# A graph attention layer on one core: one block for all stages, a third of the tile-row gathers moved behind the edge loop, the marks moved behind the projection

## The chip, the core and the metric

The kernel runs on one NeuronCore of a Trainium2 chip. Its engines work in parallel and meet only at semaphores: TensorE (PE) multiplies, VectorE (DVE), ScalarE (ACT) and GpSimd (POOL) compute, SyncE (SP) issues transfers; ACT and POOL issue transfers too. Gathers by an index (indirect DMAs) are issued by GpSimd, one instruction for 128 rows. The metric is the device time of one execution in microseconds (us), as the median of several runs.

## What is computed

x holds 12,500 nodes of 128 features. There are 212,500 edges, sorted by their destination dst. Cut to what matters:

```
h = relu(layernorm(x))
q = h @ Wq.T + bq;  k = edge_attr @ Wk.T + bk;  v = h @ Wv.T + bv      # 8 heads of 16
qs, qd = q[src], q[dst]
score = (segsoftmax(qs.k) + segsoftmax(qd.k) + segsoftmax(qs.qd)) * edge_weight ** lam
out = x + leaky_relu(segment_sum(score * v[dst], dst) @ Wo.T + bo)
```

segsoftmax is a softmax over the edges of one destination. Since dst is sorted, the kernel computes it with running maxima and running sums along the edges, and reads each node's result at its last edge.

## The kernel before

There are three stages, each in a `Block` of its own: at the end of a block every engine waits until all have come.

**Node stage** (`node_pass`). The nodes are taken in 14 steps (NSTEP) of 7 tiles (HALF), two steps to a pair. VectorE takes the statistics of step k+3 (`node_stats`), finishes those of k+2 (`normalise`), and moves step k's q and v out of PSUM (`take_qv`); ScalarE normalises and copies the turned tiles, TensorE turns and projects, SyncE stores q and v to DRAM (`q_tab`, `v_tab`). Beside it runs a search: for each of 99 columns of 128 nodes it must be known where a node's last edge stands. `mark_tiles` finds the row of 128 destinations that holds it, GpSimd gathers these rows, 11 columns to a batch (`batch`, 9 batches, 99 gathers) into two buffers of `rows_i`, and VectorE counts in each batch (`count`, two instructions). A batch can only be fetched when the count two before it is done. `marks` compares neighbouring destinations and writes masks (`pen`), offsets (`near`) and, with ScalarE's logarithm and exponential, the edge weights (`att`); SyncE then writes `near_tab` and `pa_tab` to DRAM. `marks` stands after the third pair, counts after pairs 1 to 6 and at the end of the stage.

**Edge stage** (`edge_pass`). The edges are taken in 104 units of 4 groups, a group being 4 tiles of 128 edges. GpSimd gathers q of the sources (`qsrc`, 4 gathers to a group, 1,664 in all) into a ring of 8 groups, so it can be at most 8 groups ahead of TensorE's turn of them (`qs_turned`). SyncE loads edge features, offsets, masks and windows of q. TensorE, ScalarE and VectorE form the products, sum them over heads, and scan. Before the loop VectorE does the last two counts and works out with 22 small instructions (`place`) where every node's result stands (`last_i`). After it the ends of the 128 runs of edges are joined (`join_ends`, `join_fix`), and GpSimd gathers the 128 rows to be mended (`fix`) and scatters them back.

**Result stage** (`out_pass`). GpSimd gathers the results by `last_i`, 98 gathers in 14 steps into 4 buffers (`st`); VectorE scales v, TensorE applies Wo, ScalarE stores.

GpSimd's queue is one list in program order; an instruction in it that waits holds all behind it.

Of the kernel before, what the change touches and what calls it, by code (L numbers as in the profile page):

```python
# [54 lines left out]
NB = NN // LB  # L55
TINY = 2.0 ** -63
# [9 lines left out]
def gnn_kernel(nc, x, idx, dst_rows, dst_prev, dst_first, tile_first, ea, dist, wqvT, bqv, wkT, bk, woT, bo, lam,  # L66
# [12 lines left out]
    with ExitStack() as ctx:  # L79
# [15 lines left out]
        rows_i = sb("rows_i", [P, 2, LB * P], I32)  # L95
# [3 lines left out]
        rows_in = [sem("rows_in0"), sem("rows_in1")]  # L99
        rows_used = sem("rows_used")  # L100
        le_ready = sem("le_ready")
# [7 lines left out]
        def count(dve, m):  # L109

            dve.wait_ge(rows_in[m % 2], 16 * LB * (m // 2 + 1))
            need(dve, rows_used, m)
            nc.vector.tensor_tensor(le[:, :, :], rows_i[:, m % 2, :].rearrange("p (l i) -> p l i", i=P),
# [5 lines left out]
        node_pass(nc, locals())  # L119
        edge_pass(nc, locals())  # L120
# [3 lines left out]
def node_pass(nc, env):  # L124
# [4 lines left out]
    rows_i, rows_in, rows_used, idx, idx_sb, idx_in, count = (env[k] for k in (  # L129
        "rows_i", "rows_in", "rows_used", "idx", "idx_sb", "idx_in", "count"))  # L130
# [4 lines left out]
    with ExitStack() as ctx:  # L135
# [6 lines left out]
        def sem(name):  # L142
            return ctx.enter_context(nc.semaphore(name))

# [14 lines left out]
        mine = sb("mine", [P, T])  # L159
# [5 lines left out]
        tile_i = sb("tile_i", [P, NN], I32)  # L165
        dist_sb = sb("dist_sb", [P, T])
        clipped = sb("clipped", [P, T])
        power = sb("power", [P, T])
        keep = same
# [14 lines left out]
        bits = rows_i[:, :, :].rearrange("p b n -> p (b n)").bitcast(BF16)  # L184
# [22 lines left out]
        q_out = [sem("q_out0"), sem("q_out1")]  # L207
# [3 lines left out]
        bases_in = sem("bases_in")  # L211
# [5 lines left out]
        pool_turns = sem("pool_turns0")  # L217
# [3 lines left out]
        clipped_ready = sem("clipped_ready")  # L221
        pa_ready = sem("pa_ready")
        pa_out = sem("pa_out")
        zeros_out = sem("zeros_out")
# [4 lines left out]
        block = ctx.enter_context(nc.Block())  # L229

        @block.sync
        def _(sp):
# [5 lines left out]
            def store(k, b):  # L238
                sp.wait_ge(qv_copied, 2 * k + 2)
                sp.dma_start(q_v[:, bass.ds(k * HALF * F, HALF * F)], qs[:, b, :, :]).then_inc(q_out[b], 16)  # L240
                sp.dma_start(v_v[:, bass.ds(k * HALF * F, HALF * F)], vs[:, b, :, :]).then_inc(q_out[b], 16)
# [13 lines left out]
            sp.dma_start(bases[:, :], env["tile_first"]).then_inc(bases_in, 16)  # L255
            with sp.Fori(0, NSTEP // 2 - 3) as w:
# [6 lines left out]
            sp.wait_ge(zeros_ready, 1)  # L263
            sp.dma_start(q_tab[NPAD:NPAD + P, :], zeros[:, :]).then_inc(zeros_out, 16)
# [9 lines left out]
            sp.wait_ge(near_out, 16 * NSUP)  # L274
            sp.wait_ge(pa_out, 16 * A)
            sp.wait_ge(zeros_out, 16)
            for b in range(2):
                sp.wait_ge(q_out[b], 32 * (NSTEP // 2))
            sp.wait_ge(consts, 16 * NLOAD)
            sp.wait_ge(bases_in, 16)  # L280

        @block.scalar
        def _(act):
# [38 lines left out]
            with act.Fori(1, NSTEP // 2 - 1) as w:  # L322
# [5 lines left out]
                norm_relu(2 * w + 2, 0)  # L328
            copy_turned(NSTEP - 3, 1)
# [45 lines left out]
        def _(pool):  # L375
            def batch(m):
# [11 lines left out]
            for m in range(NB):  # L388
                batch(m)
# [967 lines left out]
```

## Time and profile before

| | |
|---|---|
| median of 3 runs | 2455.67 us (2454.73 to 2461.15) |
| the profiled execution | 2454.85 us, span of its trace 2453.0 us |
| node stage, to the first instruction of the next block | 0 to 177.3 us |
| edge stage | 177.3 to 2307.7 us |
| result stage | 2307.7 to 2453.0 us |
| busy: PE, DVE, ACT, POOL | 1788.6, 1731.4, 913.2, 1770.9 us |

The span is the time from the first to the last record of one profiled execution. An engine's busy share is an average over stages with different limits, so what a change is worth is read from the stage in which it stands and from the wait that ends last there.

### The profile page before, as it was taken

What the parts mean: (1) busy time and instruction counts of PE and PEld (TensorE: products, weight loads), DVE (VectorE), ACT (ScalarE), POOL (GpSimd) and SP (SyncE); (2) the same over time, 40 slices, a digit from 0 to 9 for tenths busy, and PEclk for the clock granted to TensorE, in tenths of its full rate; (3) what the DMA queues carried; (4) which work ended last, traced back from release to release, by engine and by line L of the source; (5) the groups of instructions that cost most, each with busy time, mean ns of one, the idle gap of its engine ahead of it and who ended that gap; (6) DMA issues with size and microseconds to landing.
All of it is one profiled execution on the core that took longest, in us unless ns stands there. A gap on an engine that the chain in (4) does not pass through costs nothing. (4 is left out here: it accounts for less than half of the span.)

```text
span 2453.0 us, 42538 instructions
## 1 busy us (share of the span) xinstructions
PE 1788.6 (73%) x10766; PEld 1111.6 (45%) x10766; DVE 1731.4 (71%) x2875; ACT 913.2 (37%) x1929; POOL 1770.9 (72%) x1869
## 2 busy tenths in 40 slices
PE   5406787877777777777777878777777777778177
PEld 4404444444444444444444444444444444444155
DVE  7736677777777777777777777777777777777355
ACT  5302343434334434333333434333343333334111
POOL 4567777777777777777777777777777777776374
PEclk9758888988888888888888888889888888889566
DMA  7468777777777777777777777777777777774254
GB/s 243 151 174 253 222 224 224 227 223 234 220 227 229 225 226 240 220 232 222 223 223 225 225 223 230 226 226 231 224 237 219 228 233 225 225 224 137 102 146 158
DMA packets 395523, 527.87 MB, mean 215 GB/s; under 512 B 82285, under 2 KB 301297, under 8 KB 382178
## 3 DMA queue, kind: packets, MB, share of 16 engines
q1 hardware_dynamic: 317586, 339.87, 44.3%
q0 software_dynamic: 59616, 119.35, 19.6%
q10 hardware_dynamic: 18288, 68.29, 7.6%
q8 instruction: 11, 0.18, 0.0%
q14 instruction: 22, 0.18, 0.0%
HBM read 442.67 MB, written 84.57 MB: 215 GB/s over the span
## 5 line engine op out<-in xcount | busy, mean ns | idle before, releaser
L718 POOL DMA_INDIRECT qsrc<-q_tab,idx_sb x1664 | 1576.8, 948 | 516.2 <-issue 497.9
L777 PE MATMUL qs_ps<-ident,qsrc 128*128 128x128 f32 x1664 | 306.2, 313 | 459.4 <-DMA qsrc<-q_tab,idx_sb 450.1
L941 DVE SCALAR_TENSOR_TENSOR prod<-k_ps,bk_col,kq 128x512 f32<-128x512 f32 x416 | 309.1, 743 | 464.3 <-PE lg_ps L747 442.2
L839 ACT COPY kq<-qd_ps 128x512 f32<-128x512 f32 x416 | 242.6, 583 | 901.0 <-PE qd_ps L768 895.3
L768 PE MATMUL qd_ps<-onehot,window 128*128 128x128 f32 x3328 | 525.3, 311 | 4.5 <-DVE onehot L931 4.5
L777 PEld LDWEIGHTS qs_ps<-ident,qsrc 128*128 128x128 f32 x1664 | 198.0, 155 | 725.7 <-issue 678.7
L757 PE MATMUL k_ps<-ea_sb,wk_sb 128*128 128x512 f32 x832 | 481.4, 664 | 55.3 <-DMA ea_sb<-in_ea 55.3
L945 DVE TENSOR_TENSOR prod<-qs_ps,kq 128x1024 f32<-128x1024 f32 x416 | 505.3, 1215 | 0.0
L768 PEld LDWEIGHTS qd_ps<-onehot,window 128*128 128x128 f32 x3328 | 490.4, 226 | 6.1 <-issue 6.1
L833 ACT ACTIVATE kq<-k_ps,bk_col 128x512 f32<-128x512 f32 x416 | 286.0, 688 | 213.0 <-PE k_ps L757 145.2
L747 PE MATMUL lg_ps<-prod,heads 128*32 128x384 f32 x3328 | 357.9, 503 | 1.5 <-DVE prod L945 1.5
L931 DVE TENSOR_SCALAR_CACHE_REDUCE onehot<-near_sb,node_col 128x512 f32<-128x512 bf16 x416 | 306.2, 736 | 0.0
L747 PEld LDWEIGHTS lg_ps<-prod,heads 128*32 128x32 f32 x3328 | 66.6, 109 | 358.2 <-issue 188.2
L788 PE MATMUL t_ps<-ident,sums 128*128 128x128 f32 x936 | 193.0, 324 | 14.9 <-ACT rows L863 12.1
L977 DVE TENSOR_TENSOR_SCAN sums<-max_ps,terms 128x387 f32<-128x387 f32 x208 | 189.0, 950 | 3.6
L757 PEld LDWEIGHTS k_ps<-ea_sb,wk_sb 128*128 128x128 f32 x832 | 147.9, 222 | 55.7 <-DMA ea_sb<-in_ea 55.7
L863 ACT COPY rows<-t_ps 128x384 f32<-128x384 f32 x312 | 148.4, 476 | 6.2 <-PE t_ps L788 6.2
L381 POOL DMA_INDIRECT rows_i<-in_dst_rows,tile_i x99 | 99.0, 1000 | 69.0 <-issue 54.0
L788 PEld LDWEIGHTS t_ps<-ident,sums 128*128 128x128 f32 x936 | 133.7, 167 | 27.1 <-issue 10.6
L1188 POOL DMA_INDIRECT st<-state,last_i x98 | 92.8, 947 | 38.8 <-issue 29.6
L956 DVE TENSOR_TENSOR_SCAN max_ps<-pa_sb,lg_ps 128x387 f32<-128x387 f32 x104 | 100.4, 965 | 25.1 <-ACT terms L846 24.6
L851 ACT COPY sums<-max_ps 128x387 f32<-128x387 f32 x104 | 50.0, 481 | 133.0 <-DVE max_ps L956 133.0
(147 smaller groups left out, 1034.9 us busy)
## 6 DMA issues: line engine op xcount, KB each, us to landing
ea_sb<-in_ea SPq DMA_DIRECT2D x104, 1024.0 KB
window<-q_tab SPq DMA_DIRECT2D x1664, 64.0 KB
state<-rows ACTq DMA_DIRECT2D x104, 576.0 KB
near_sb<-near_tab SPq DMA_DIRECT2D x104, 512.0 KB
pa_sb<-pa_tab SPq DMA_DIRECT2D x104, 258.0 KB
qsrc<-q_tab,idx_sb POOLq DMA_INDIRECT x1664
xs<-in_x SPq DMA_DIRECT2D x28, 448.0 KB, 5.4
q_tab<-qs SPq DMA_DIRECT2D x14, 448.0 KB, 2.7
```

The costliest lines, as they stand in the source:

```text
L718: pool.indirect_dma_start(out=qsrc[:, r, j, :], out_offset=None, in_=q_tab, in_offset=bass.IndirectOffsetOnAxis(ap=idx_sb[:, q, g * GRP + ...
L747: t = nc.tensor.matmul(lg_ps[2 * SUP * j:2 * SUP * (j + 1), :, 1:W1], heads[:, g, :], prod[:, m % 2, :, j * P:(j + 1) * P], start=g == 0, ...
L757: nc.tensor.matmul(k_ps[:, m % 2, :], wk_sb[:, :], ea_sb[:, p, g * GRP * P:(g + 1) * GRP * P], start=True, stop=True).then_inc(k_ready, 1)
L768: t = nc.tensor.matmul(qd_ps[:, at], window[:, r, j, :], onehot[:, m % 2, at], start=True, stop=True)
L777: t = nc.tensor.transpose(qs_ps[:, m % 2, j * P:(j + 1) * P], qsrc[:, r, j, :], ident[:, :])
L788: t = nc.tensor.transpose(t_ps[:, a * P:(a + 1) * P], sums[:, b, k, a, 1:W1], ident[:, :])
L833: nc.scalar.activation(kq[:, m % 2, 0, :], k_ps[:, m % 2, :], ACT.Identity, bias=bk_col[:, 0:1]).then_inc(k_copied, 1)
L839: nc.scalar.copy(kq[:, m % 2, 1, :], qd_ps[:, :]).then_inc(qd_copied, 1)
L931: nc.vector.tensor_scalar(onehot[:, m % 2, :].rearrange("p (j i) -> p j i", j=GRP), near_sb[:, p, :, :].rearrange("p (j g) i -> p g j i", ...
L941: nc.vector.scalar_tensor_tensor(out=prod[:, g % 2, 2, :], in0=k_ps[:, g % 2, :], scalar=bk_col[:, 0:1], in1=kq[:, g % 2, 1, :], op0=ALU.a ...
L945: nc.vector.tensor_tensor(prod[:, g % 2, 0:2, :], qs_ps[:, g % 2, :].unsqueeze(1).to_broadcast([P, 2, GRP * P]), kq[:, g % 2, :, :], ALU.m ...
L977: s = nc.vector.tensor_tensor_scan(sums[:, b, k, :, :].rearrange("p a i -> p (a i)"), max_ps[:, :, :].rearrange("p a i -> p (a i)"), terms ...
```

## The change

1. **One block.** All three stages stand in one `Block`. Instead of the two common ends each engine waits on named semaphores: SyncE, TensorE, ScalarE and VectorE wait in `nodes_done` (all of the node stage's work and stores, `pa_tab` included) before the edge stage, and in `edges_done` (results stored, ends joined, `fix` scattered, `edge_step` 40) before the result stage. GpSimd has waits of its own: only `q_out` (q is in DRAM) and `zeros_out` before the edge stage, and before the result stage `fix_out`, `edge_step` 20 and `rows_used` 6.
2. **Gathers.** `rows_i` has four buffers. Batches 0 to 5 (NEARLY = 6; 66 gathers) are fetched in the node stage, batches 6, 7 and 8 (33) behind the edge loop: 6 and 7 before the `fix` gather, 8 between that and the scatter. The result buffers `st` lie in the first two buffers of `rows_i`.
3. **Counts.** Counts 0 and 1 stand after pairs 3 and 4, counts 2 to 5 in the first four units of the edge loop, 6 before `join_ends`, 7 and 8 after `join_fix`. `place` is done in two parts: for 65 columns in the fourth unit, for 33 at the end.
4. **Marks** stand behind the last pair, with `near` and `clipped` earlier in them. `pa_tab` is written from ScalarE's queue, its first two parts before the logarithm. The zeros of `q_tab` are written early.
5. q and v stores have semaphores of their own (`q_out`, `v_out`).

The diff, cut to its core:

```diff
+NEARLY = 6
+BUF = (0, 1, 2, 3, 0, 1, 2, 3, 2)
+PLACED = NEARLY * LB - 1
...
+        def fetch_rows(pool, m, tile_i):
+
+            if BUF[m] in BUF[:m]:
+                pool.wait_ge(rows_used, max(k for k in range(m) if BUF[k] == BUF[m]) + 1)
+            pool.sem_inc(rows_turns, 1)
+            for j in range(LB):
+                pool.indirect_dma_start(out=rows_i[:, BUF[m], j * P:(j + 1) * P], out_offset=None, in_=dst_rows,
...
+        block = ctx.enter_context(nc.Block())
+
+        nodes_done = node_pass(nc, locals())
+        edges_done = edge_pass(nc, locals())
...
@@ node_pass, sync
-            sp.wait_ge(pa_ready, 3)
-            for a in range(A - 1):
-                sp.dma_start(pa_tab[:, :, a * W1:(a + 1) * W1], pa[:, :, 0, :]).then_inc(pa_out, 16)
-            sp.dma_start(pa_tab[:, :, (A - 1) * W1:], pa[:, :, :, :].rearrange("p c k i -> p c (k i)")
-                         ).then_inc(pa_out, 16)
...
@@ node_pass, scalar
+            act.wait_ge(pen_ready, 1)
+            act.wait_ge(pa_heads, 2)
+            for a in range(A - 1):
+                act.dma_start(pa_tab[:, :, a * W1:(a + 1) * W1], pa[:, :, 0, :]).then_inc(pa_out, 16)
             act.wait_ge(clipped_ready, 1)
             nc.scalar.activation(clipped[:, :], clipped[:, :], ACT.Ln).then_inc(ln_ready, 1)
             act.wait_ge(ln_ready, 1)
             nc.scalar.activation(power[:, :], clipped[:, :], ACT.Exp, scale=lam_sb[:, 0:1]).then_inc(power_ready, 1)
+            act.wait_ge(pa_ready, 1)
+            act.dma_start(pa_tab[:, :, (A - 1) * W1:], pa[:, :, :, :].rearrange("p c k i -> p c (k i)")
+                          ).then_inc(pa_out, 16)
...
@@ node_pass, gpsimd
-            for m in range(NB):
-                batch(m)
+            pool.wait_ge(tiles_ready, 2)
+            for m in range(NEARLY):
+                fetch_rows(pool, m, tile_i)
...
@@ node_pass, vector
             for w in range(1, NSTEP // 2):
                 pair(w, min(2, 2 * (NSTEP // 2 - 1 - w) - 1))
-                if w == 2:
-                    marks()
-                count(dve, w - 1)
-            dve.wait_ge(step, 18)
+                if w == 3 or w == 4:
+                    count(dve, w - 3)
+            marks()
+            dve.wait_ge(step, 17)
             dve.wait_ge(power_ready, 1)
             nc.vector.tensor_tensor(att, by_chunk(power[:, :]), by_chunk(keep[:, :]), ALU.mult).then_inc(pa_ready, 1)
-            count(dve, NB - 3)
...
@@ edge_pass, gpsimd
+            for b in range(2):
+                pool.wait_ge(env["q_out"][b], 16 * (NSTEP // 2))
+            pool.wait_ge(env["zeros_out"], 16)
             over_units(pool, unit)
 
+            for m in range(NEARLY, NB - 1):
+                fetch_rows(pool, m, tile_i)
             for b in range(2):
                 pool.wait_ge(rows_out[b], 16 * (NCOL // 2))
...
+            fetch_rows(pool, NB - 1, tile_i)
             pool.wait_ge(fixed_ready, 1)
...
+            pool.wait_ge(edge_step, 20)
+            pool.wait_ge(env["rows_used"], NEARLY)
             pool.wait_ge(fix_out, 16)
+            pool.sem_inc(pool_turns, 1)
+            for k in range(RST):
+                fetch_results(pool, k)
...
@@ edge_pass, vector
+                    if early and g == 2:
+                        count(dve, NEARLY - QUAD + q)
+                    if early and q == QUAD - 1 and g == 2:
+                        dve.wait_ge(env["rows_used"], NEARLY)
+                        place(0, PLACED, 0)
...
+            count(dve, NEARLY)
             join_ends()
             join_fix()
+            for m in range(NEARLY + 1, NB):
+                count(dve, m)
+            dve.wait_ge(env["rows_used"], NB)
+            place(PLACED, NT, 20)
```

**Where the instructions stand.** In the rows below each is one instruction, or a run of equal ones (x10), with its line and the semaphores that it waits for. First GpSimd from the last batch of the node stage to the first source gathers, before:

```order
L381 DMA rows_i<-in_dst_rows,tile_i 128x128 [waits tiles_ready,rows_used]
L381 DMA rows_i<-in_dst_rows,tile_i 128x128 x10
L135 UNCONDITIONAL_BRANCH
L707 UNCONDITIONAL_BRANCH [waits barrier_Pool_Activation_PE_DVE_SP_gather]
L718 DMA qsrc<-q_tab,idx_sb 128x128 [waits idx_in0]
L718 DMA qsrc<-q_tab,idx_sb 128x128 x15
```

and in the change (L138 is `fetch_rows`, L147 `fetch_sources`; line numbers are the changed kernel's):

```order
L138 DMA rows_i<-in_dst_rows,tile_i 128x128 [waits rows_used]
L138 DMA rows_i<-in_dst_rows,tile_i 128x128 x10
L755 UNCONDITIONAL_BRANCH
L147 DMA qsrc<-q_tab,idx_sb 128x128 [waits idx_in0,zeros_out,q_out0,q_out1]
L147 DMA qsrc<-q_tab,idx_sb 128x128 x15
```

The common end of the block between them is gone; the first source gather waits for the stores of q instead, and 33 row gathers that stood ahead of it do so no more.

Then GpSimd behind the edge loop, before, from the last source gathers to the first results:

```order
L718 DMA qsrc<-q_tab,idx_sb 128x128 x3
L728 DMA fix<-state,fix_i 128x72 [waits rows_out1,rows_out0]
L732 DMA state<-fixed,fix_i 212992x72 [waits fixed_ready]
L547 UNCONDITIONAL_BRANCH [waits fix_out]
L1181 UNCONDITIONAL_BRANCH [waits barrier_Pool_Activation_PE_DVE_SP_gather]
L1188 DMA st<-state,last_i 128x72 x28
```

and in the change, from the end of batch 6 on (L156 is `fetch_results`, its target lies in `rows_i`):

```order
L138 DMA rows_i<-in_dst_rows,tile_i 128x128 x10
L138 DMA rows_i<-in_dst_rows,tile_i 128x128 [waits rows_used]
L138 DMA rows_i<-in_dst_rows,tile_i 128x128 x10
L774 DMA fix<-state,fix_i 128x72 [waits rows_out1,rows_out0]
L138 DMA rows_i<-in_dst_rows,tile_i 128x128 [waits rows_used]
L138 DMA rows_i<-in_dst_rows,tile_i 128x128 x10
L779 DMA state<-fixed,fix_i 212992x72 [waits fixed_ready]
L156 DMA rows_i<-state,last_i 128x72 [waits fix_out,edge_step,rows_used]
L156 DMA rows_i<-state,last_i 128x72 x27
L1251 UNCONDITIONAL_BRANCH
L156 DMA rows_i<-state,last_i 128x72 [waits node_step1]
```

Batches 6 and 7 have come in ahead of the `fix` gather, batch 8 between that and the scatter; the common end behind the scatter is gone, and the first 28 result gathers follow it directly.

Last VectorE at the end of the node stage, before (two counts, the weights `att`, a third count, the common end), and at the start of the edge stage:

```order
L113 TENSOR_TENSOR le<-rows_i,nid 128x1408 [waits rows_used,rows_in1]
L117 TENSOR_REDUCE cnt<-le 128x11 [waits le_ready]
L535 TENSOR_TENSOR pa<-power,same 128x13x128 [waits power_ready,step]
L113 TENSOR_TENSOR le<-rows_i,nid 128x1408 [waits rows_used,rows_in0]
L117 TENSOR_REDUCE cnt<-le 128x11 [waits le_ready]
L135 UNCONDITIONAL_BRANCH
L919 UNCONDITIONAL_BRANCH [waits barrier_Pool_Activation_PE_DVE_SP_release]
L113 TENSOR_TENSOR le<-rows_i,nid 128x1408 [waits rows_used,rows_in1]
L117 TENSOR_REDUCE cnt<-le 128x11 [waits le_ready]
L113 TENSOR_TENSOR le<-rows_i,nid 128x1408 [waits rows_used,rows_in0]
L117 TENSOR_REDUCE cnt<-le 128x11 [waits le_ready]
L1104 SCALAR_TENSOR_TENSOR last_f<-tile_f,cnt 128x99 [waits rows_used]
```

and in the change, first where the node stage ends, then in the first unit of the edge loop:

```order
L546 CAST fix_i<-at_f 128x1 [waits step]
L569 TENSOR_TENSOR pa<-power,same 128x13x128 [waits power_ready,step]
L973 UNCONDITIONAL_BRANCH
L976 MEMSET held 128x8x3 [waits q_out1,v_out0,v_out1,q_out0,zeros_out,pa_ready,near_out,qv_copied,pa_out,hT_copied,h_ready]
L1000 TENSOR_TENSOR prod<-qs_ps,kq 128x1024 [waits qs_turned]
L126 TENSOR_TENSOR le<-rows_i,nid 128x1408 [waits rows_used,rows_in2]
L130 TENSOR_REDUCE cnt<-le 128x11 [waits le_ready]
L986 TENSOR_SCALAR onehot,picked<-near_sb,node_col 128x512 [waits qd_ready,near_in1]
```

VectorE now waits for the stores (`pa_out` among them) instead of the common end, and counts inside the loop's units, between the products and the next mask.

## Rows read from the trace of the kernel before

**Rows 1.** The page: busy time by engine; granted TensorE clock in 40 slices.
```profile
PE 1788.6 (73%) x10766; PEld 1111.6 (45%) x10766; DVE 1731.4 (71%) x2875; ACT 913.2 (37%) x1929; POOL 1770.9 (72%) x1869
...
PEclk9758888988888888888888888889888888889566
```

**Rows 2.** The page's costliest groups: line, engine, count, busy, mean ns, idle before.
```profile
L718 POOL DMA_INDIRECT qsrc<-q_tab,idx_sb x1664 | 1576.8, 948 | 516.2 <-issue 497.9
```

**Rows 3.** Windows, core 0: length, busy by engine, granted clock, DMA share, GB/s.
```profile
190.00:200.00 10.00, 5.71 (x30) 4.94 (x31) 6.68 (x14) 1.86 (x3) 7.56 (x9) 0.78 1.04 308
...
300.00:1000.00 700.00, 547.31 (x3395) 330.31 (x3395) 516.63 (x806) 278.34 (x596) 529.74 (x559) 0.86 0.75 226
```

**Rows 4.** Timeline of GpSimd: start, length, instruction, what ended the idle time.
```profile
88.87 2.25 POOL L381 DMA_INDIRECT rows_i<-in_dst_rows,tile_i  x1 [0.30 <-issue]
...
178.07 1.88 POOL L718 DMA_INDIRECT qsrc<-q_tab,idx_sb  x1 [9.15 <-POOLq L135]
...
181.50 1.83 POOL L718 DMA_INDIRECT qsrc<-q_tab,idx_sb  x1 [0.30 <-issue]
```

**Rows 5.** Timeline of GpSimd, end of the edge stage and start of the results.
```profile
2260.92 0.94 POOL L718 DMA_INDIRECT qsrc<-q_tab,idx_sb  x1 [0.30 <-issue]
2288.24 0.94 POOL L728 DMA_INDIRECT fix<-state,fix_i  x1 [26.38 <-DMA state<-rows]
2298.30 0.98 POOL L732 DMA_INDIRECT state<-fixed,fix_i  x1 [9.12 <-DVE fixed L1045]
2308.47 0.97 POOL L1188 DMA_INDIRECT st<-state,last_i  x1 [9.19 <-POOLq L547]
```

**Rows 6.** Timeline of VectorE in the node stage.
```profile
34.58 1.44 DVE L438 BATCH_NORM_STATS2 stats<-xs 128x6 f32<-128x128 f32 x7
...
45.32 1.61 DVE L113 TENSOR_TENSOR le<-rows_i,nid 128x1408 f32<-128x1408 int32 x1
...
48.50 1.44 DVE L438 BATCH_NORM_STATS2 stats<-xs 128x6 f32<-128x128 f32 x7
...
60.74 1.88 DVE L473 TENSOR_TENSOR same<-dst_i 128x1664 f32<-128x1664 int32 x1
...
73.57 1.62 DVE L113 TENSOR_TENSOR le<-rows_i,nid 128x1408 f32<-128x1408 int32 x1
...
88.69 1.62 DVE L113 TENSOR_TENSOR le<-rows_i,nid 128x1408 f32<-128x1408 int32 x1
...
107.96 1.44 DVE L438 BATCH_NORM_STATS2 stats<-xs 128x6 f32<-128x128 f32 x7
...
121.34 1.63 DVE L113 TENSOR_TENSOR le<-rows_i,nid 128x1408 f32<-128x1408 int32 x1
...
130.21 1.61 DVE L113 TENSOR_TENSOR le<-rows_i,nid 128x1408 f32<-128x1408 int32 x1
```

**Rows 7.** Timeline of SyncE's queue: issues, start and length.
```profile
138.43 3.65 SPq L272 DMA_DIRECT2D pa_tab<-pa  x1
177.32 0.37 SPq L679 DMA_DIRECT2D near_sb<-near_tab  x1
...
179.38 9.15 SPq L692 DMA_DIRECT2D window<-q_tab  x16
```

**Rows 8.** The tiles pa_tab, then q_tab, in the node stage: issue to landing.
```profile
DMA to landing us min/median/max: 7.9/14.0/19.5
...
DMA to landing us min/median/max: 2.5/2.7/4.2
```

**Rows 9.** Timelines of TensorE and VectorE as the edge stage begins.
```profile
184.52 2.08 PE L757 MATMUL k_ps<-ea_sb,wk_sb 128*128 128x512 f32 x2 [55.29 <-DMA ea_sb<-in_ea]
...
190.09 0.21 DVE L1099 CAST last_i<-edge_f 128x98 int32<-128x98 f32 x1
```

**Rows 10.** Timeline of ScalarE: logarithm and exponential of the distances.
```profile
122.09 1.28 ACT L335 ACT_TABLE_LOAD   x1
...
126.29 1.68 ACT L337 ACTIVATE power<-clipped,lam_sb 128x1664 f32<-128x1664 f32 x1
```

More of the change, by code:

```diff
@@ L94, in gnn_kernel @@
         cnt = sb("cnt", [P, NN])
-        rows_i = sb("rows_i", [P, 2, LB * P], I32)
+        qsrc = sb("qsrc", [P, RING, GRP, F])
+        q_in = [sem(f"q_in{r}") for r in range(RING)]
+        rows_i = sb("rows_i", [P, 4, LB * P], I32)
+        st = rows_i[:, 0:2, :].rearrange("p b n -> p (b n)").bitcast(F32)[:, 0:RST * HALF * ROW].rearrange(
+            "p (r t k) -> p r t k", r=RST, t=HALF)
+        st_in = [sem(f"st_in{r}") for r in range(RST)]
         le = sb("le", [P, LB, P])
@@ L98, in gnn_kernel @@
         idx_in = [sem(f"idx_in{q}") for q in range(QUAD)]
-        rows_in = [sem("rows_in0"), sem("rows_in1")]
+        rows_in = [sem(f"rows_in{r}") for r in range(4)]
         rows_used = sem("rows_used")
+        rows_turns = sem("rows_turns")
+        bases_in = sem("bases_in")
+        q_out = [sem("q_out0"), sem("q_out1")]
+        zeros_out = sem("zeros_out")
+        tile_i = sb("tile_i", [P, NN], I32)
         le_ready = sem("le_ready")
@@ L227, in node_pass @@
         zeros_ready = sem("zeros_ready")
-        block = ctx.enter_context(nc.Block())
+        block = env["block"]
         @block.sync
@@ L321, in _, with pair @@
             norm_relu(2, 0)
-            with act.Fori(1, NSTEP // 2 - 1) as w:
+            def pair(w):
                 copy_turned(2 * w - 1, 1)
@@ L328, in _ @@
                 norm_relu(2 * w + 2, 0)
+            with act.Fori(1, NSTEP // 2 - 1) as w:
+                pair(w)
             copy_turned(NSTEP - 3, 1)
@@ L603, in edge_pass @@
         pa_in = [sem(f"pa_in{q}") for q in range(QUAD)]
-        q_in = [sem(f"q_in{r}") for r in range(RING)]
         window_in = [sem(f"window_in{r}") for r in range(RING)]
@@ L671, in _ @@
         def _(sp):
+            env["nodes_done"](sp)
+            sp.wait_ge(env["bases_in"], 16)
             def unit(h, q):
@@ L803, in unit @@
                         sums_of_heads(h, q, g - 1)
+            env["nodes_done"](pe)
             keys(0, 0, 0)
@@ L896, in unit @@
                         exps(v)
+            env["nodes_done"](act)
             act.wait_ge(ones_ready, 3)
@@ L920, in _ @@
         def _(dve):
+            env["nodes_done"](dve)
             nc.vector.memset(held[:, :, 0, :], -BIG).then_inc(ones_ready, 1)
@@ L1046, in join_fix, with place @@
                                         ).then_inc(fixed_ready, 1)
-            def place(m0, m1):
+            def place(m0, m1, done):
+                c0, c1 = (m0 + 1 if m0 else 0), m1 + 1
+                nc.vector.scalar_tensor_tensor(out=last_f[:, c0:c1], in0=tile_f[:, c0:c1], scalar=float(P),
+                                               in1=cnt[:, c0:c1], op0=ALU.mult, op1=ALU.add).then_inc(step, 1)
+                dve.wait_ge(step, 2 if m0 else 1)
+                nc.vector.tensor_tensor(has[:, m0:m1], last_f[:, m0 + 1:m1 + 1], last_f[:, m0:m1], ALU.is_gt)
                 n = [edge_f[:, k, m0:m1] for k in range(8)]
@@ L1156, in out_pass @@
         pool_turns = sem("pool_turns2")
-        st_in = [sem(f"st_in{r}") for r in range(RST)]
         step = [sem(f"node_step{i}") for i in range(4)]
```

205 lines of the change are left out of this document (104 added, 101 removed).

## The prediction

> **What bounds the kernel now.** I read the page first. No engine is busy over 73% of the span [rows 1], so I asked which one never pauses where the time goes. The costliest group is GpSimd's 1,664 source gathers: 948 ns each, and the 516 us of idle time before them is "issue" in pieces of 0.30 us, not waiting [rows 2]. The timeline of GpSimd says the same: the first gather starts at 178.07 and the last at 2260.92 [rows 4, 5], so 1,663 steps took 2082.85 us, 1.2525 us each. A group of 4 gathers is 5.01 us, a unit 20.04 us. In the window from 300 to 1000 us, 34.9 units, TensorE was busy 547 us and VectorE 517 us [rows 3]: 15.7 and 14.8 us of each unit's 20.04. So **the edge stage lasts as long as GpSimd's issuing**, and the end of the kernel moves with the start of the first source gather, unless the others run so late that the ring of 8 groups fills.
>
> That gather started at 178.07 because the block had ended: the row gathers ran until 168.9, then GpSimd idled 9.15 us, released by the block's end [rows 4]. Behind the loop the chain is: last source gather ends at 2261.86 (call it E), `fix` at E+26.4, scatter at E+36.4 (VectorE's `fixed` released it), first result gather at E+46.6 after 9.19 us at the block's end [rows 5]; from there to the end of the span 144.5 us.
>
> **When the first source gather can start.** It now needs batch 5 issued and q stored.
> Pairs, from VectorE's timeline [rows 6]: pair 1 from 34.58 to 45.32, 10.74 us with no count ahead of it. A count takes 48.50 - 45.32 = 3.18. Pair 2 took 12.24 (48.50 to 60.74), pair 3 11.9 (from 73.57 + 3.18 to 88.69), pair 4 12.9 (from 88.69 + 3.18 to 107.96 - 3.18), pair 5 13.38, pair 6 5.69 (from 121.34 + 3.18 to 130.21), with a count ahead of each. `marks` took 73.57 - 60.74 = 12.83.
> New order: 45.32, pairs 2 and 3 like pair 1 (66.8), count 0 (70.0), pair 4 as after a count, 12.24 (82.2), count 1 (85.4), pair 5 at 13.38 (98.8), pair 6 between 5.69 and 8.87, since no count hides its wait for TensorE; I take 7.3. The projection ends at **106.1**. Bounds: all pairs at 10.74 and the short end, 100.3; each pair as slow as measured, 111.3. The last q store lands 2.7 us after its issue (2.5 to 4.2) [rows 8]; with 0.2 chosen for the semaphores q is there at 109.0.
> Batch 5 waits for count 1 (85.4) and takes 11 x 1.2525 = 13.8: done at 99.2, early enough; its slack is 10 us. The early zeros cost nothing here: they are hidden behind the projection.
> First source gather: **109.0 instead of 178.07, -69.1 us.**
>
> **Can the others follow?** Marks run from 106.1 to 118.9. ScalarE's logarithm and exponential took 5.88 from 122.09 to the end of the last [rows 10]; they start six instructions into marks and end about with them; `att` (1.9 us, as the equally long `same`, L473 [rows 6]) ends near 121.5. The last part of `pa_tab` then lands 7.9 to 19.5 us after its issue; 19.5 was behind the two other parts, which now go out some 10 us earlier, from ScalarE's queue [rows 7, 8]. I take 10: `nodes_done` at 131.5, bounds 129.4 and 141.0. From SyncE's first issue (177.32) to TensorE's first keys was 7.2 us (184.52), the keys took 2.08 [rows 7, 9]; with 2 us for mask, pick and turn, an estimate from the same row, group 0 is turned 11.3 us after `nodes_done`: **142.8** (140.7 to 152.3). GpSimd fills 8 groups in 32 x 1.2525 = 40.1 us, until 149.1. So it does not stall at the start by this estimate, by up to 3 us at the bound. SyncE's windows (9.15 us for a unit's 16 [rows 7]) are faster than 20 us.
> Then the first units carry counts: VectorE needs 14.8 + 3.2 = 18.0 us in each of three and 18.0 + 6.1 in the fourth (`place` took from 184.2 to 190.3, the end of L1099 [rows 9]; for 98 columns, so this is an upper bound for 65): 78 us against GpSimd's 80. The lead is kept and nothing is added. Where that cover is gone, each further microsecond of lateness costs one.
>
> **What slows GpSimd itself.** A row gather at 88.87 took 2.25 instead of 0.94 us [rows 4]: VectorE's compare of a count ran from 88.69 to 90.31 [rows 6], and the gather ended 0.81 us after it. Two source gathers at the start (1.88 and 1.83 us) lie beside the two counts there [rows 4]: 1.83 us lost, already in the 2082.85. All these instructions of VectorE read two tiles of SBUF. With such an instruction of 1.62 us a gather loses about 1.0, with one of 1.88 about 1.25. New beside source gathers: `near`, `mine`, `att` (3 x 1.25) and four counts (4 x 1.0), 7.75 - 1.83 = **+5.9**. Bounds: 0 and 11.
> The Trainium skill, SBUF — State Buffer, section Who interferes with whom, says that a VectorE instruction with two SBUF inputs contends only with a GpSimd instruction that reads SBUF, and infers that descriptor generation is not stalled by it; by that the sum would be 5.9 us lower. The row speaks against the inference.
>
> **Behind the loop.** Batches 6 and 7: 22 gathers, E+0.3 to E+27.9, plus 1.0 beside count 6, so `fix` at E+28.9 instead of E+26.4. The join does not feel it: its path goes over the ends that SyncE loads. `fix` and batch 8: 12 x 1.25 = 15.0, E+43.9, plus 1.0 beside count 7: the scatter at E+44.9 instead of E+36.4, though `fixed` is there at E+36.4. It ends at E+45.9. Its landing has no row of its own: the nearest are the q stores (2.5 to 4.2 from issue [rows 8]), the upper end is the whole 9.19 us that GpSimd sat at the block's end [rows 5]. I take 2.8: first result gather at E+48.7, **+2.1** (bounds +1 and +9). So the 9 us saved at this block's end are spent on batch 8.
> VectorE's count 8 waits for batch 8 (about E+47), then 3.2 and at most 6.1 for the second `place`: E+57. Only then do SyncE, TensorE, ScalarE and VectorE enter the result stage. The first step's 7 gathers are issued by E+57.5 anyway, and GpSimd needs the first buffer back at E+48.7 + 28 x 1.25 = E+83.8. Hidden by 20 us; the rest stays 144.5.
>
> **Sum.** -69.1 + 5.9 + 2.1 = -61.1. Span 2453.0 - 61.1 = 2391.9; the profiled execution had 1.85 us around its span and was 0.8 us below the median of the runs shown: 2391.9 + 1.85 + 0.8 = **2395 us**.
>
> **Rivals.**
> *The ring fills (0.14).* Group 0 is late and TensorE stays at its lower clock: the third slice of the page (123 to 184 us) has the granted clock at 5 tenths, its lower level, after a stretch in which TensorE had nothing to do [rows 1]; it was 0.78 from 190 to 200 and 0.86 later [rows 3]. TensorE's 3.92 us a group at 0.86 is at most 6.7 at 0.50; 16 groups would take 107 us against GpSimd's 80, so some 27 less the 6 to 9 of lead: +18, 2413. Against it: the same cold start recovered within 10 us.
> *The projection does not speed up (0.09).* Pairs as slow as with counts: 111.3 instead of 106.1, 2400.
> *The entry to the results is late (0.06).* The scatter's landing costs the full 9 us: +7, 2402.
> *No contention at the counts (0.04).* The gather beside a count would lose nothing: -5.9 -1 -1 = 2387. This is the mechanism of the page named above.
> *The start is early but worth nothing (0.03).* GpSimd fills the ring and waits for the same late `nodes_done` as before (177): then 2453 - 177.32 + 11.3 is the consumers' path and they catch up on the ring only: about the time of before, 2450 to 2458. It would take a `pa_tab` that lands 46 us late; its longest was 19.5.
> *Slower (0.02).* TensorE becomes the bound of the loop through its clock. 3.92 x 0.86 / c reaches 5.01 us at c = 0.673; the gain of 61 us over 416 groups is 0.147 a group, gone at c = 0.654. At 0.60 it is 5.62 us a group: +193 us net of the gain, about 2650. Nothing in the rows brings the clock of the loop down from 0.86.
>
> **How the numbers follow.** The forecast has 0.62, with a range of its own from 2386 (projection at 100.3, half the contention) to 2404 (projection at 111.3, some 4 us later behind the loop). A difference of 0.3%, 7.4 us, is about what a measurement of this kernel can tell from none. Faster: 0.62 + 0.14 + 0.09 + 0.06 + 0.04 = 0.95. Same: 0.03, the start worth nothing. Slower: 0.02. The range goes from 2384 (early projection, little contention) to 2413 (the ring fills).
>
> **What would show it.** The first source gather near 109, with one gap before it and none at a common end; `nodes_done` 20 us later; GpSimd's gathers without gaps over 0.4 us from then to the last, at about 2198; seven gathers of 1.6 to 2.8 us by the early counts and marks; the scatter at E+45, the first result at E+49. It is wrong if GpSimd waits for TensorE's turns around 150 us, if the mean of a gather rises above 0.95 us, or if the result stage is longer than 145 us.

## The result, and the profile after

The changed kernel took **2396.32 us** (median of 4 runs, 2391.21 to 2402.75), the kernel before 2456.81 us beside it (4 runs, 2454.73 to 2461.15). The ratio is 0.9753, with a 95% interval from 0.9725 to 0.9781: faster by 60 us, where 61 less were predicted (2395). Measured again in a later set of runs it was 2398.25 us (2394.02 to 2402.97) against 2454.67, ratio 0.9769 (0.9749 to 0.9790). Eight of the experiments ran on two chips on which the kernel before itself took 3269.51 and 3327.28 us, so their totals are compared only with those.

The profiled execution took 2398.02 us, its span was 2396.2 us, 56.8 less than before. The page has the same work in a shorter span; the third slice of the granted clock, 5 tenths before [rows 1], is 7:

```profile
PE 1795.9 (75%) x10766; PEld 1111.0 (46%) x10766; DVE 1734.8 (72%) x2897; ACT 914.0 (38%) x1929; POOL 1778.5 (74%) x1869
...
PEclk9878988888888988989888888888888888888566
```

GpSimd's three lists of gathers among the costliest groups (line, engine, count, busy, mean ns, idle before; answers to [rows 2]):

```profile
L147 POOL DMA_INDIRECT qsrc<-q_tab,idx_sb x1664 | 1586.3, 953 | 516.7 <-issue 502.0
...
L138 POOL DMA_INDIRECT rows_i<-in_dst_rows,tile_i x99 | 96.8, 978 | 49.2 <-issue 29.3
...
L156 POOL DMA_INDIRECT rows_i<-state,last_i x98 | 93.1, 950 | 31.7 <-issue 29.6
```

The 516.7 us of idle time are the same 0.30 us pieces as before. What moved is when the list starts. GpSimd's timeline at the end of batch 5, the first source gathers, and the last one (answers to [rows 4]):

```profile
101.98 0.95 POOL L138 DMA_INDIRECT rows_i<-in_dst_rows,tile_i  x1 [0.30 <-issue]
112.41 0.95 POOL L147 DMA_INDIRECT qsrc<-q_tab,idx_sb  x1 [9.48 <-DMA q_tab<-qs]
113.66 2.14 POOL L147 DMA_INDIRECT qsrc<-q_tab,idx_sb  x1 [0.30 <-issue]
116.11 1.46 POOL L147 DMA_INDIRECT qsrc<-q_tab,idx_sb  x1 [0.30 <-issue]
117.87 1.50 POOL L147 DMA_INDIRECT qsrc<-q_tab,idx_sb  x1 [0.30 <-issue]
...
122.18 2.63 POOL L147 DMA_INDIRECT qsrc<-q_tab,idx_sb  x1 [0.31 <-issue]
...
2204.97 0.95 POOL L147 DMA_INDIRECT qsrc<-q_tab,idx_sb  x1 [0.30 <-issue]
```

VectorE beside it (answers to [rows 6]): the marks begin at 109.03, so there the projection ends. `near`, `mine` and `att` (the lines L510, L520 and L569) are the three instructions beside which slow gathers were foreseen. The slow gather at 116.11 is a fourth: it begins while L518 runs, an instruction with one input in SBUF, and ends 0.82 us after it. The first source gather, at 112.41, begins while L509 runs and is not slow. After `att` VectorE waits 11.87 us for `pa_tab`.

```profile
109.03 1.88 DVE L506 TENSOR_TENSOR same<-dst_i 128x1664 f32<-128x1664 int32 x1
...
111.00 1.89 DVE L509 TENSOR_SCALAR pa<-same 128x1664 f32<-128x1664 f32 x1
112.81 1.88 DVE L510 TENSOR_TENSOR near<-dst_i 128x1664 bf16<-128x1664 int32 x1
...
115.72 1.03 DVE L518 TENSOR_SCALAR dist_sb<-dist_sb 128x1664 f32<-128x1664 f32 x1
116.67 1.88 DVE L520 TENSOR_TENSOR mine<-dst_i,nfirst 128x1664 f32<-128x1664 int32 x1
...
122.09 1.89 DVE L569 TENSOR_TENSOR pa<-power,same 128x1664 f32<-128x1664 f32 x1
135.85 0.08 DVE L976 MEMSET held<- 128x24 f32 x1 [11.87 <-DMA pa_tab<-pa]
```

And the start of TensorE's part (answers to [rows 9]):

```profile
143.53 2.04 PE L809 MATMUL k_ps<-ea_sb,wk_sb 128*128 128x512 f32 x2 [35.48 <-DMA ea_sb<-in_ea]
...
147.07 1.10 PE L829 MATMUL qs_ps<-ident,qsrc 128*128 128x128 f32 x8
```

Group 0 is turned about 148.1. The 33rd source gather, the first that needs a group's place in the ring again, starts at 156.38 after the usual 0.30 us. The others began 36 us behind GpSimd and it did not wait for them.

Behind the loop, GpSimd (answers to [rows 5]); E is now 2205.92:

```profile
2227.88 2.05 POOL L138 DMA_INDIRECT rows_i<-in_dst_rows,tile_i  x1 [0.30 <-issue]
...
2235.23 0.95 POOL L774 DMA_INDIRECT fix<-state,fix_i  x1 [0.31 <-issue]
...
2243.99 2.12 POOL L138 DMA_INDIRECT rows_i<-in_dst_rows,tile_i  x1 [0.30 <-issue]
...
2251.41 0.98 POOL L779 DMA_INDIRECT state<-fixed,fix_i  x1 [0.30 <-issue]
2254.53 0.97 POOL L156 DMA_INDIRECT rows_i<-state,last_i  x1 [2.14 <-DMA state<-fixed,fix_i]
```

`fix` at E+29.3, scatter at E+45.5, first result at E+48.6. The scatter waits for nothing: `fixed` was written by 2243.75 (E+37.8), and batch 8 stood ahead of it in the list.

The balance of the two spans: first source gather 112.41 instead of 178.07, -65.66; the 1,663 steps from first to last source gather 2092.56 instead of 2082.85 us, +9.71; from the last source gather to the first result 49.56 instead of 47.55, +2.01; from there to the end 141.67 instead of 144.53, -2.86. Sum -56.8.

### The profile page after: what moved, and what is told of

The parts are those of the page before. It is cut to its first block, busy times and chain, and to the rows that moved or that the text cites. A ratio compares the mean times of both kernels' runs of the same rounds, so it can differ in the third digit from the quotient of the medians.

```text
span 2396.2 us, 42567 instructions
## 1 busy us (share of the span) xinstructions
PE 1795.9 (75%) x10766; PEld 1111.0 (46%) x10766; DVE 1734.8 (72%) x2897; ACT 914.0 (38%) x1929; POOL 1778.5 (74%) x1869
## 3 DMA queue, kind: packets, MB, share of 16 engines
q0 software_dynamic: 59616, 119.35, 20.2%
## 4 chain that ended last, share of the span: by engine, by line
POOL 58%; issue 20%; PE 10%; DVE 5%; DMA 5%; ACT 1%; POOLq 1%; ACTq 0%; DVEq 0%; SPq 0%
POOL qsrc L147 53%; DMA qsrc<-q_tab,idx_sb 3%; POOL rows_i L156 3%; PE qd_ps L820 2%; PE k_ps L809 2%; POOL rows_i L138 1%; PE lg_ps L799 1%; PE qs_ps L829 1%; PE qv_ps L394 1%; DVE prod L1000 1%; PE t_ps L840 1%; ACT hb L334 1%; DMA pa_tab<-pa 0%; POOLq L66 0%; DVE prod L996 0%
## 5 line engine op out<-in xcount | busy, mean ns | idle before, releaser
L147 POOL DMA_INDIRECT qsrc<-q_tab,idx_sb x1664 | 1586.3, 953 | 516.7 <-issue 502.0
L1000 DVE TENSOR_TENSOR prod<-qs_ps,kq 128x1024 f32<-128x1024 f32 x416 | 505.3, 1215 | 0.0
L138 POOL DMA_INDIRECT rows_i<-in_dst_rows,tile_i x99 | 96.8, 978 | 49.2 <-issue 29.3
L1011 DVE TENSOR_TENSOR_SCAN max_ps<-pa_sb,lg_ps 128x387 f32<-128x387 f32 x104 | 100.3, 965 | 30.9 <-ACT terms L899 28.6
L156 POOL DMA_INDIRECT rows_i<-state,last_i x98 | 93.1, 950 | 31.7 <-issue 29.6
```

The costliest lines, as they stand in the source:

```text
L147: pool.indirect_dma_start(out=qsrc[:, r, j, :], out_offset=None, in_=q_tab, in_offset=bass.IndirectOffsetOnAxis(ap=idx_sb[:, q, g * GRP + ...
L1000: nc.vector.tensor_tensor(prod[:, g % 2, 0:2, :], qs_ps[:, g % 2, :].unsqueeze(1).to_broadcast([P, 2, GRP * P]), kq[:, g % 2, :, :], ALU.m ...
```

## The experiments

### Does the end move one for one with the first source gather?

The theory of the prediction: GpSimd's list sets the time, so a later first source gather costs what it is late. The rival: GpSimd's early start only fills its ring, and the time hangs on when the other engines start. Four edits move one against the other. In the first GpSimd waits for the whole node stage, as the others do:

```diff
-            for b in range(2):
-                pool.wait_ge(env["q_out"][b], 16 * (NSTEP // 2))
-            pool.wait_ge(env["zeros_out"], 16)
+            env["nodes_done"](pool)
             over_units(pool, unit)
```

> The changed kernel, but GpSimd waits for all of the node stage (nodes_done, pa_tab included) before the source gathers, like the other engines. Theory (the start of the first source gather sets the end): it starts near 136.2 instead of 112.4 us, +23.8, and no longer meets the three long VectorE instructions of marks (3.9 us lost beside them in the changed kernel's trace): +19.9, about 2416 us. Rival (the other engines' start at 135.8 sets the pace of the loop and the ring only hides it): no change, 2396.

The second does `marks()` after the third pair (`if w == 2`), as before, in place of behind the last:

> The changed kernel with marks back after the third pair, all else kept. Theory: the projection ends some 13.5 us later (marks took 12.8 us, and the pipeline refills), so the first source gather is near 126; near and mine no longer meet source gathers: -2.3. In all about +11, 2407 us. nodes_done hardly moves (near 134). Rival (the start of the other engines sets the time): no change, 2396.

The third fetches and counts all 9 batches ahead of the edge loop, and nothing behind it:

```diff
-            for m in range(NEARLY):
+            for m in range(NB):
                 fetch_rows(pool, m, tile_i)
...
-                    if early and g == 2:
-                        count(dve, NEARLY - QUAD + q)
...
-            for m in range(NEARLY, NB - 1):
-                fetch_rows(pool, m, tile_i)
```

> The changed kernel with all nine batches of row gathers and all counts ahead of the edge loop, still in one block. Theory: batch 8 has to wait for count 6 and ends near 148, so the first source gather starts near 148.7 instead of 112.4, +36; no count lies in the loop, -2.6; behind the loop nothing stands between fix and scatter, the first result gather comes at E+39.9 instead of E+48.6, -8.7: about +25, 2421 us. If batch 8 behind the loop costs nothing there (rival), the last term is missing: about 2430.

The fourth delays only the others, by 8 reductions of VectorE behind the marks, ahead of `att`:

```diff
+            for i in range(8):
+                nc.vector.tensor_reduce(nfirst[:, 0:1], mine[:, :], AX_X, ALU.add).then_inc(step, 1)
+                dve.wait_ge(step, 18 + i)
             dve.wait_ge(power_ready, 1)
```

> The changed kernel with eight more reductions (1.89 us each, 15.1 us, one SBUF input) on VectorE ahead of att, so that all but GpSimd enter the edge stage 15 us later. In the changed kernel GpSimd's gather into the first slot of the ring that has to be free again starts at 156.4, the slot was free at 148.1: 8.3 us of cover. Theory: the excess over the cover shows, +7, about 2403 us. Rival 1 (no cover is left in later units, one for one): +15, 2411. Rival 2 (the ring is never full): 2396.

These four ran where the kernel before took 3269.51 us (31 runs): 3264.44, 3274.49, 3254.65 and 3257.56 us (10 runs each), ratios 0.9975 (0.9938 to 1.0012), 1.0034 (1.0003 to 1.0065), 0.9961 (0.9926 to 0.9995), 0.9979 (0.9956 to 1.0001). All four expectations (2396 to 2421 us) missed by over 800 us, and not through the edits: the kernel before, unedited, was as slow there. The changed kernel itself was not run on that chip. In the first one's list of costliest groups GpSimd's idle time is 1245.4 us, of which only 457.3 are its own pace; the largest part of the rest, 381.0 us, is put down to the loads of the gathers' indices (`idx_sb`), which SyncE issues:

```profile
L147 POOL DMA_INDIRECT qsrc<-q_tab,idx_sb x1664 | 1577.0, 948 | 1245.4 <-issue 457.3
```

and a stretch of its chain that ended last (start, length, what) has a hole of the length of half a unit:

```profile
1041.17 0.66 DVE onehot L984 x2
1041.83 9.62 another core or an unknown queue
1051.48 0.05 DVEq L66
```

From 1049.9 to 1051.5 none of TensorE, VectorE, ScalarE and GpSimd is at work in this trace; VectorE had stood since 1041.8, ScalarE since 1043.1, TensorE since 1046.3. From 300 to 1000 us GpSimd issued 416 source gathers, a unit in 26.9 us instead of 20. So GpSimd was not what bounds the loop there. In that condition the first source gather came at 181.96, 181.48, 204.22 and 162.90 in the four, and the time did not follow: the one with the latest start has the lowest median. Nor did it follow the start of the others: VectorE's `held`, its first instruction of the edge stage, came at 181.13, 192.29, 212.11 and 198.42, and again the latest has the lowest median. So these four runs decide nothing between theory and rival; what bounds the loop there stays open.

The changed kernel and the first edit were therefore run again together:

> The changed kernel itself, beside the kernel before on the same chip. Two earlier sets of runs had the kernel before at 3270 and 3327 us instead of 2457, with TensorE, VectorE, ScalarE and GpSimd at rest together for some 10 us in each unit of the edge loop. If this chip is like the one of the result: 2396 us, ratio 0.975, first source gather at 112. If it is like those: GpSimd is not the engine that sets the loop there, so an early first gather only fills its ring; the ratio should be 0.994 to 1.000 and the first source gather near 163.

> As the first experiment: before its first source gather GpSimd waits for all of the node stage (pa_tab and near_tab too), not for q alone. If this chip is like the one of the result and my theory holds (the end moves one for one with the first source gather): the gather starts at about 136 instead of 112, hence 2396 + 24 less the slow gathers beside near, mine and att (3 x 1.25) = 2416 us, ratio 0.983. Rival: TensorE's start sets the loop, and GpSimd's early start is cover only: 2396, ratio 0.975. If the chip is like the two others: 0.994 to 1.000 whatever the theory.

Here the kernel before took 2454.67 us. The changed kernel took 2398.25 us (0.9769). With the wait for the whole stage it took **2414.16 us** (2409.70 to 2416.69), ratio 0.9825 (0.9809 to 0.9842). GpSimd's timelines, of the change and of this one:

```profile
110.83 0.94 POOL L147 DMA_INDIRECT qsrc<-q_tab,idx_sb  x1 [9.51 <-DMA q_tab<-qs]
```

```profile
132.42 0.94 POOL L147 DMA_INDIRECT qsrc<-q_tab,idx_sb  x1 [30.75 <-DMA pa_tab<-pa]
```

21.6 us later at the start; 4.8 less in the steps (4.0 of it because the plain step is 1.2485 instead of 1.2509 us, and only 0.8 from slow gathers, where I had expected 3.75); 0.4 less behind the loop; 3.8 more in the result stage; together +20.2, the difference of the spans (2414.8 and 2394.6). The others started 2.4 us earlier here than in the change (VectorE's `held` at 131.59 and 133.95), and the kernel is slower all the same. That refutes the rival: it gives 2396, and all four runs lie above 2409. The closeness to the expected 2416 is partly luck: the plain step (-4.0) and the result stage (+3.8), neither of which the expectation had, cancel.

The third edit was also run again, with the numbers worked out anew:

> The change without its moved gathers: all 9 batches are fetched ahead of the edge loop, and all counts stand in the node stage; one block, named waits and marks behind the projection stay. If this chip is like the one of the result and GpSimd's list sets the time: 33 more gathers stand ahead of the first source gather, 41 us, of which the 9.5 us that it waits for q hide some, and each batch has to wait for a count; the first source gather starts at about 160, with the counts out of the loop's way. Behind the loop fix waits for the join and the scatter comes at E+36 instead of E+45, the first result at E+40 instead of E+49. 2398 + 48 - 9 - 4 less contention = 2433 us, ratio 0.991 (from the first set I had said 2421, before I had the waits between batches). Rival: the moved gathers gave nothing, since they cost behind the loop what they save ahead of it: 2398, ratio 0.977. If the chip is like the two slower ones: within 1% of the kernel before.

It took **2424.27 us** (2423.65 to 2425.01) against 2456.80, ratio 0.9872 (0.9855 to 0.9888). GpSimd's timeline:

```profile
156.14 0.94 POOL L147 DMA_INDIRECT qsrc<-q_tab,idx_sb  x1 [0.30 <-issue]
...
2266.46 0.94 POOL L774 DMA_INDIRECT fix<-state,fix_i  x1 [26.31 <-DMA state<-rows]
2276.53 1.00 POOL L778 DMA_INDIRECT state<-fixed,fix_i  x1 [9.13 <-DVE fixed L1103]
2279.67 0.97 POOL L156 DMA_INDIRECT rows_i<-state,last_i  x1 [2.14 <-DVE edge_i L1146]
```

Against the changed kernel beside the other set: start +45.3, steps -9.7, to the first result -9.0, result stage +1.1, sum +27.7, again the difference of the spans (2422.3 and 2394.6). So the 33 moved gathers are worth 26 us: ahead of the loop they cost 45.3 us, less 9.7 since neither counts nor marks are left to stand beside source gathers (5.6) and the plain step is short again (4.0); behind it they cost 9.0, because 26 us of GpSimd's waiting for the join cover most of them there. Without the 4.0 us of the plain step, which nothing here explains, they would be worth some 30. My second estimate had counted 48 us for the start and only 4 for the steps and was 9 too high; the first, 2421, was nearer. What remains without them, 2456.8 - 2424.3 = 32.5 us, is the share of all that this version keeps: the single block, the named waits, the marks behind the projection, the four buffers and the moved stores of `pa_tab` and the zeros. The parts of these 32.5 us were not told apart, since the second and fourth edit ran only where GpSimd is not the bound.

### What slows a gather beside VectorE?

Theory: a gather that stands beside a VectorE instruction with two inputs in SBUF ends only after it. Rival, an inference of the Trainium skill, SBUF — State Buffer, section Who interferes with whom: the generation of descriptors is not held up by such an instruction. Two kernels put one more instruction of VectorE into each of the 100 units after the first four, equally long, with two inputs in SBUF or with one:

```diff
+                    if not early and g == 1:
+                        nc.vector.tensor_tensor(le[:, :, :], rows_i[:, 1, :].rearrange("p (l i) -> p l i", i=P),
+                                                nid[:, 0:LB].unsqueeze(2).to_broadcast([P, LB, P]), ALU.is_le)
```

> The changed kernel with one more compare of VectorE (two SBUF inputs, 1.62 us, the same as in a count) in each of the last 100 units of the edge loop; its result is not used. VectorE has 5 us free in a unit of 20. Theory (GpSimd cannot begin a gather while such an instruction runs): a gather that falls into it loses on average 0.87 us (between 0.24 and 1.49), so +87 us, about 2483 (2420 to 2545). Rival (the inference that descriptor generation is not stalled by a two-input tensor_tensor): 2396.

```diff
+                    if not early and g == 1:
+                        nc.vector.tensor_reduce(spare[:, :], le[:, :, :], AX_X, ALU.add)
```

> The control to the run with a compare in each unit: there one more reduction of VectorE of the same length (1.62 us, one SBUF input), result not used. Theory: no gather loses anything, 2396, within 3 us. Rival (it is VectorE's longer unit that costs, not the second input): the same increase as with the compare.

Where they ran the kernel before took 3327.28 us (23 runs), and they 3317.80 and 3328.88 us (one run each), so the totals say nothing on GpSimd. The traces do. From the costliest groups, with compares:

```profile
L147 POOL DMA_INDIRECT qsrc<-q_tab,idx_sb x1664 | 1658.0, 996 | 1211.9 <-issue 475.9
...
L1048 DVE TENSOR_TENSOR le<-rows_i,nid 128x1408 f32<-128x1408 int32 x100 | 161.7, 1617 | 0.0
```

and with reductions:

```profile
L147 POOL DMA_INDIRECT qsrc<-q_tab,idx_sb x1664 | 1580.5, 950 | 1288.3 <-issue 467.3
...
L1048 DVE TENSOR_REDUCE spare<-le 128x11 f32<-128x1408 f32 x100 | 160.9, 1609 | 0.0
```

With the same 161 us of VectorE the gathers are busy 77.5 us longer beside compares, 0.78 us for each. From the two timelines: 98 gathers began while a compare ran, took 1.75 us on average and ended 0.79 us after it; 78 that began before one and ended during it took 0.94. Of the gathers that began while a reduction ran, 130, the mean is 0.95 us. One pair of the compares' trace, VectorE and then GpSimd:

```profile
1039.97 1.61 DVE L1048 TENSOR_TENSOR le<-rows_i,nid 128x1408 f32<-128x1408 int32 x1
```

```profile
1040.56 1.83 POOL L147 DMA_INDIRECT qsrc<-q_tab,idx_sb  x1 [0.30 <-issue]
```

That settles it for this kernel: the theory holds, and the inference of the Trainium skill does not. The rule of the Trainium skill, same section, that on this chip a reduction never contends agrees with the 0.95 us. Two limits: which part of a gather's work is held up, reading its indices from SBUF or writing the descriptors, no run here separates; and two inputs are not the only cause, as the gather beside L518 shows (1.46 us). The size needs a word: 0.78 us is the mean over all phases (0.87 had been expected); a gather that begins early in the compare loses more, one that begins at its end less.

### Can the gathers behind the loop be brought off the path?

After the change the scatter waits for batch 8, not for `fixed`. Two versions give batch 6 a buffer of its own, issue 7 of its gathers in the time in which GpSimd waits for q, and put only 5 gathers between `fix` and the scatter; the second also does count 7 ahead of the join:

```diff
-BUF = (0, 1, 2, 3, 0, 1, 2, 3, 2)
+BUF = (0, 1, 2, 3, 0, 1, 4, 3, 2)
...
+            fetch_rows(pool, NEARLY, tile_i, 0, 7)
...
-            for m in range(NEARLY, NB - 1):
-                fetch_rows(pool, m, tile_i)
+            fetch_rows(pool, NEARLY, tile_i, 7, LB)
+            fetch_rows(pool, NEARLY + 1, tile_i)
+            fetch_rows(pool, NEARLY + 2, tile_i, 0, 6)
...
-            fetch_rows(pool, NB - 1, tile_i)
+            fetch_rows(pool, NB - 1, tile_i, 6, LB)
```

> The changed kernel with a fifth buffer for rows: 7 gathers of batch 6 are issued in GpSimd's idle time ahead of the first source gather (9.5 us in the changed kernel), and batch 8 is split, 6 gathers ahead of fix and 5 behind it. Theory: the first source gather stays at 112.4, the scatter comes at E+36.5 instead of E+45.2, the first result gather at E+40 instead of E+48.6, and GpSimd sets the result stage: -8.7, about 2387.5 us. Rival (the entry of the other engines sets the result stage; VectorE ends its counts and place near E+49 instead of E+55): -5, 2391.

> As the split kernel, and count 7 stands before join_ends, where VectorE waits 6.1 us for the ends in the changed kernel. Theory (GpSimd sets the result stage): no further gain, 2387.5, or 1 us worse, since the compare meets a gather. Rival (the entry of the others sets it): 3.2 us better than the split alone.

Beside the 3327.28 us of before they took 3311.01 and 3305.89 us (12 runs each), ratios 0.9959 (0.9932 to 0.9987) and 0.9941 (0.9913 to 0.9968); the two cannot be told apart. The second was run again:

> A version meant to beat the change: 7 gathers of batch 6 fill the 9.5 us in which GpSimd waits for q, batch 8 is split so that 5 of its gathers stand behind fix, and count 7 is done ahead of the join. Behind the loop 26 + 1 gathers instead of 33 + 1: the scatter can go at about E+37 (when fixed is there) instead of E+45.4, so 2398 - 8.8 = 2389.5 us or, if one slow gather less stands beside a count, 2388; ratio 0.973. Rival: fixed comes later because count 7 stands ahead of the join (3.2 us): 2392, ratio 0.9745. Rival: the added gathers delay the first source gather by what they save: 2398, ratio 0.977. If the chip is like the two slower ones: within 1% of the kernel before.

It took **2389.70 us** (2384.97 to 2392.67) against 2456.80, ratio 0.9735 (0.9718 to 0.9751). GpSimd's timeline:

```profile
111.04 2.53 POOL L138 DMA_INDIRECT rows_i<-in_dst_rows,tile_i  x1 [0.30 <-issue]
113.87 1.46 POOL L147 DMA_INDIRECT qsrc<-q_tab,idx_sb  x1 [0.30 <-issue]
...
2238.06 0.98 POOL L781 DMA_INDIRECT state<-fixed,fix_i  x1 [0.74 <-DVE fixed L1108]
2241.18 0.97 POOL L156 DMA_INDIRECT rows_i<-state,last_i  x1 [2.14 <-DMA state<-fixed,fix_i]
```

Now `fixed` releases the scatter, at E+37.0, and the first result comes 8.4 us sooner behind the last source gather. The second rival, that the added gathers delay the first source gather, was right in part: two of the 7 added gathers stand beside marks and took 2.27 and 2.53 us, so the first source gather starts 3.0 us later than without them; in exchange those losses are gone from the source gathers (steps 6.5 us shorter, 4.0 of it the plain step). The first rival was not: `fixed` was written at E+36.7, 1.1 us earlier than in the change, though count 7 stands ahead of it. The medians are 8.6 us apart, by 0.9735 against 0.9769 for the change, with intervals that overlap slightly at 0.975; the two were not run on one chip. That the scatter no longer waits for batch 8 is shown (8.4 us); that this version beats the changed one by some 8 us is likely, and as much as 4 us of that is the plain step, which nobody aimed at.

## Why the prediction was right, point by point

**The bound.** GpSimd's list sets the end: shown by the wait for the whole stage and by the gathers put back, where the spans differ by what the start, the steps and the tail differ. It holds only where the other engines keep up; on the two slower chips GpSimd itself had to wait.

**First source gather**, predicted 109.0: 112.41. The projection ended at 109.03 instead of 106.1; q took 3.4 us from there instead of 2.9. Batch 5 was done at 102.9 (99.2), and GpSimd had 9.5 us of slack (10). Within the bounds (100.3 to 111.3 for the projection).

**The others follow**: `nodes_done` at 135.85 (131.5, bounds 129.4 to 141.0), group 0 turned at 148.1 (142.8, bounds 140.7 to 152.3). GpSimd's lead held, and none of the 1,663 source gathers behind the first began more than 0.4 us after the end of the one before: the rival of the full ring (0.14) did not come.

**What slows GpSimd**, +5.9 predicted, +9.7 measured: the step that was mis-sized. In sum the slow gathers cost what was said: with all steps under 1.27 us taken as plain, the excess of the others rose from 6.6 to 12.2 us, +5.6. By part it is luck: four gathers beside marks lost 3.9 (three, 3.75), four beside the early counts 2.4 (4.0), and shorter delays elsewhere grew by 1.2, which the prediction had put at nothing. But the plain step also rose, from 1.2485 to 1.2510 us, which over 1,663 steps is +4.0, and the mean of a gather to 953 ns, above the 0.95 that I had named as a sign of being wrong. The second run of the change shows the same (1.2509), the three variants run with or after it do not (1.2485). It goes with the program and not with the chip: the median gather is 947 ns in both traces of the change and in the kernel with reductions, 944 or 945 in all others, among them the kernel with compares on the chip of the one with reductions. What in the program lengthens a plain step by 2.4 ns is open.

**Behind the loop**, +2.1 predicted, +2.0 measured: `fix` at E+29.3 (E+28.9), scatter at E+45.5 (E+44.9), first result at E+48.6 (E+48.7). The landing of the scatter, chosen as 2.8 between ends far apart, is 2.14 us after the issue ends.

**The result stage**, predicted unchanged: 2.9 us shorter. From the first to the last result gather both took the same, 121.45 and 121.76 us; the difference lies behind the last one, where the granted clock (the third number from the end) was 0.65 before and 0.75 after. Windows of before, then of after:

```profile
2429.92:2453.00 23.08, 14.86 (x54) 10.40 (x53) 9.68 (x11) 4.33 (x5) 0.94 (x1) 0.65 0.22 84
```

```profile
2376.29:2396.20 19.91, 11.61 (x49) 8.60 (x47) 9.68 (x11) 4.33 (x5) 0.95 (x1) 0.75 0.25 96
```

In the four kernels run later this stretch is 19.87, 23.98, 21.22 and 20.24 us with clocks of 0.75, 0.64, 0.69 and 0.67: it goes roughly with the clock. Whether the clock goes with the change is not shown: both traces of the changed kernel have 0.75, the kernel before and the three variants 0.64 to 0.69, one trace each.

**The sum**: -56.8 instead of -61.1 in the span, 4.3 us off; that the median came out only 1.3 from the forecast is partly luck: the start was 3.4 us and the steps 3.8 us worse than said, and the result stage, predicted unchanged, gave 2.9 back. Besides, the profiled execution was now 1.7 us above the median, where the forecast had it 0.8 below.

## What to carry to other kernels

When one engine's list of instructions never pauses, look for what stands in that list ahead of the part that matters, and move it behind a wait that the list has anyway: here 33 gathers cost 45 us ahead of the loop, 10 of which the loop made good, and 9 us behind it. Let that engine wait for its own input alone instead of for a whole stage; it cost 16 us to do otherwise. Then ask what is late next: here it was the scatter behind the moved gathers, and splitting one batch brought it off the path.

## What was not expected of the hardware

A gather by index that begins while VectorE runs an instruction with two inputs in SBUF ends about 0.8 us after that instruction (98 cases); beside a reduction as long it takes its 0.95 us (130 cases). It holds for short ones too: in the loop of the changed kernel, from 1000 to 1600 us, the 12 gathers that began while L1027 ran (0.55 us, `terms` and `pa_sb`, both in SBUF) took 1.09 us on average, the 107 that began beside L1000 (1.21 us, one input from PSUM) 0.947. One input can do it too: L518 of the marks (`TENSOR_SCALAR`, 1664 elements in 1.03 us) stood beside a newly begun gather in ten of the traces, and in each the gather took 1.45 or 1.46 us and ended 0.81 or 0.82 us after it, while the gathers that began beside L509, as many elements in 1.89 us, took 0.94 or 0.95 us in the same ten. What makes the difference between these two no experiment here tested.

On two chips the same kernel before took 3270 and 3327 us instead of 2455, with instructions of the same length (a gather 948 ns, a multiplication by VectorE 1.21 us) and with waits of an engine of up to 10 us for which the trace names no releaser: between 1000 and 1200 us of the first experiment ScalarE had 13 such waits, 71.9 us. All four compute engines stood still together for at most 3.1 us at a time (from 300 to 2900 us), not for some 10 us as one of the expectations says. What stops them was not found; no variant of the change gained more than 0.6% there, so an edit that shortens GpSimd's list is judged only beside a kernel before that GpSimd bounds.
